# A selective-scan tower on one core: one channel tile's product with B moves from VectorE and GpSimd to TensorE

## What is computed

```python
# D_INNER = 512 channels, D_STATE = 16 states
def step(h, inp):
    dt_t, xv_t, B_t, C_t = inp
    dA = jnp.exp(dt_t[:, :, None] * A[None])
    h = dA * h + (dt_t * xv_t)[:, :, None] * B_t[:, None, :]
    y_t = jnp.einsum('bdn,bn->bd', h, C_t)
    return (h, y_t)
```

## Time and profile before

| | |
|---|---|
| three runs of the kernel | 2601.56, 2601.98, 2603.1 us; median 2601.98 us |
| the profiled execution | 2608.96 us, its span 2607.2 us |
| PE busy | 2079.5 us (80%) |
| DVE busy | 2095.7 us (80%) |
| ACT busy | 1367.9 us (52%) |
| POOL busy | 1210.5 us (46%) |
| scan stage of the first turn | from the first product with B on DVE at 393.61 us to the last gate's start at 604.23 us |

### The profile page before, as it was taken

The page is one execution under the profiler, slowest core; times in us unless marked ns, Lnnn a source line. Parts: engine busy times, 40 slices in busy tenths (PEclk is TensorE's granted clock), DMA queues, the critical chain, the costliest instruction groups (busy, mean ns, idle before and its releaser), DMA issues.

```text
span 2607.2 us, 24235 instructions
## 1 busy us (share of the span) xinstructions
PE 2079.5 (80%) x8436; PEld 1119.4 (43%) x8436; DVE 2095.7 (80%) x2435; ACT 1367.9 (52%) x1914; POOL 1210.5 (46%) x567
## 2 busy tenths in 40 slices
PE   2998886778799887777879898777878988777786
PEld 0326662225433665223542376422353246543244
DVE  6865879996786588999688467999888747799977
ACT  0563456664265446665527544666453744556644
POOL 1220248993222025999222111799722211289952
PEclk9999898999899988899989998899989999888999
DMA  5300000000220000000032000000003100000000
GB/s 182 90 14 1 1 1 1 0 1 0 70 86 1 1 1 0 1 0 0 1 101 55 1 1 1 0 0 0 0 1 118 38 1 1 1 0 0 1 0 17
DMA packets 41073, 51.27 MB, mean 20 GB/s; under 512 B 9072, under 2 KB 32368, under 8 KB 40944
## 3 DMA queue, kind: packets, MB, share of 16 engines
q1 hardware_dynamic: 40944, 49.62, 6.1%
HBM read 26.25 MB, written 10.49 MB: 14 GB/s over the span
## 4 chain that ended last, share of the span: by engine, by line
PE 45%; DVE 25%; POOL 16%; ACT 7%; issue 5%; DMA 1%; SPq 0%; POOLq 0%; DVEq 0%; ACTq 0%
PE psum L988 12%; PE psum L698 10%; POOL big L1985 10%; POOL big L1974 5%; PE psum L845 5%; ACT big L1100 4%; PE psum L833 3%; PE psum L818 3%; PE psum L761 3%; DVE mid L1733 3%; DVE big L1511 2%; DVE mid L1455 2%; PE psum L1003 2%; ACT mid L1100 2%; DVE negmax L1563 2%
## 5 line engine op out<-in xcount | busy, mean ns | idle before, releaser
L988 PE MATMUL psum<-big,ident 128*128 128x512 f32 x992 | 520.6, 674 | 186.0 <-POOL big L1985 185.7
L1835 DVE TENSOR_TENSOR_SCAN big<-psum,b,big 128x512 f32<-128x512 f32 x512 | 618.3, 1277 | 2.3 <-ACT psum L1100 2.0
L1100 ACT ACTIVATE big<-psum 128x1024 f32<-128x1024 f32 (+2 forms) x592 | 448.5, 777 | 229.1 <-PE psum L833 145.1
L1985 POOL TENSOR_TENSOR big<-big 128x2048 f32<-128x2048 f32 x124 | 561.8, 4531 | 9.1 <-DVE big L1835 9.1
L1100 ACT ACTIVATE psum<-mid,aneg 128x512 f32<-128x512 f32 x512 | 353.9, 692 | 251.3 <-DVE big L1835 251.2
L988 PEld LDWEIGHTS psum<-big,ident 128*128 128x128 f32 x992 | 202.0, 213 | 464.2 <-POOL big L1985 243.0
L1563 DVE TENSOR_REDUCE negmax<-psum 128x1 f32<-128x512 f32 x512 | 318.6, 678 | 48.7 <-PE psum L818 47.7
L1974 POOL TENSOR_TENSOR big<-mid,big 128x512 f32<-128x512 f32 (+1 forms) x128 | 224.3, 1753 | 28.2 <-ACT big L1100 28.2
L818 PE MATMUL psum<-mid 96*128 96x512 bf16 x512 | 189.4, 390 | 34.7 <-DMA mid<-mid 23.7
L833 PE MATMUL psum<-mid 98*128 98x512 bf16 x512 | 181.6, 381 | 20.1 <-ACT big L1100 14.2
L1100 ACT ACTIVATE mid<-mid 128x513 f32<-128x513 f32 (+3 forms) x120 | 104.3, 883 | 162.8 <-DVE mid L1845 88.7
(11 more groups left out here) (213 smaller groups left out, 3538.2 us busy)
## 6 DMA issues: line engine op xcount, KB each, us to landing
mid<-mid SPq DMA_DIRECT2D x192, 64.0 KB, 2.5
mid<-scratch SPq DMA_DIRECT2D x192, 64.0 KB, 2.2
scratch<-big SPq DMA_DIRECT2D x4, 1536.0 KB, 5.7
out<-hres SPq DMA_DIRECT2D x8, 513.0 KB, 7.5
big<-in_x SPq DMA_DIRECT2D x8, 512.0 KB, 5.0
big<-in_w SPq DMA_DIRECT2D x2, 1024.0 KB, 6.3
big<-in_wg SPq DMA_DIRECT2D x1, 1024.0 KB, 9.7
big<-in_wu SPq DMA_DIRECT2D x1, 1024.0 KB, 11.5
```

The costliest lines, as they stand in the source:

```text
L988: mm = nc.tensor.matmul(y_psum[:, c], ident[:, :], st(1, k)[:, c], start=(n == 0), stop=(n == NS - 1))
L1100: return nc.scalar.activation(o, a, func, **kw)
L1835: V.tensor_tensor_scan(st(0, k)[:, c], a_psum(DT * k + c), st(0, k)[:, c], b0[:, p, n, c:c + 1], ALU.mult, ALU.add).then_inc(scanned, 1)
L1985: G.tensor_tensor(st(1, k), st(0, k), c_row(k).unsqueeze(1).broadcast_to([P, DT, S]), ALU.mult).then_inc(hc_ready, 1)
```

## The change

For most steps (`by_pe(k)`: all but k = 0, 1, 16, 17 and 31, so 27 of 32) channel tile 3 is handled in another way, and DVE has two tiles of the product with B in each of these steps and POOL one:

- The product of tile 3 with B is made by PE. Once for each sequence PE transposes tile 3 of dt x (`turn_dtx`, four 128x128 transposes into `c_psum`), and ACT copies the result to SBUF (`dtx_t`). For each such step ACT makes four diagonal 128x128 matrices from the identity, scaled with B of 128 tokens (`make_diagonal`), and PE multiplies each transposed block by its diagonal (`multiply_b`) into `c_psum`, which is free once ACT has copied the row of C.
- The scan of tile 3 reads its product from `c_psum`, and its decay from SBUF (`decay_pe`). Only three decays of such a step go through the two PSUM banks.
- `spread_c` of the next step must wait until the scan of tile 3 has read `c_psum`. It is moved behind the first of the four products of `add_y`, and `multiply_b` stands ahead of the last of them.
- The fill `first` also turns B to one column for each state and 128 tokens (eight small products), and ACT copies that (`b_t`).

```diff
+def by_pe(k):
+
+    return k % NS > 1 and k < PAIR * NS - 1
+
+
+PE_STEPS = [k for k in range(PAIR * NS) if by_pe(k)]
+
+IN_BANKS = [DT * k + c for k in range(PAIR * NS) for c in range(DT) if not (by_pe(k) and c == DT - 1)]
...
+            return DT - 2 if by_pe(k) else DT - 1 - k % 2
+
+        def b_end(k):
+            return DT - 1 if by_pe(k) else DT
+
+
+        o_pe = 2 * W8 + 2 * KT * T + 2 * DT * T
+
+        def dtx_t(p):
+            return big[:, o_pe + p * S:o_pe + (p + 1) * S].rearrange("p (q m) -> p q m", q=QT)
+
+        b_t = big[:, o_pe + 2 * S:o_pe + 2 * S + PAIR * QT * NS].rearrange("p (b q n) -> p b q n", b=PAIR, q=QT)
+
+        def diagonal(k):
+            o = (o_pe + 2 * S + PAIR * QT * NS, 6 * W4)[k % 2]
+            return big[:, o:o + S].rearrange("p (q m) -> p q m", q=QT)
+
+        def decay_pe(k):
+            o = 6 * W4 + (1 + k % 2) * S
...
         def a_psum(j):
-            o = (4 + j % 2) * BANK
+            o = (4 + IN_BANKS.index(j) % 2) * BANK
             return psum[:, o:o + BANK]
+
+        def decays(j):
+            return a_psum(j) if j in IN_BANKS else decay_pe(j // DT)
...
+                pe.wait_ge(bc_split, 6 * PAIR)
+                for p in range(PAIR):
+                    for q in range(QT):
+                        o = PAIR * 32 + (QT * p + q) * NS
+                        mm = nc.tensor.matmul(flat_slot("first", 0)[:, o:o + NS], bcp[:, p, 1 + q * P:1 + (q + 1) * P],
+                                              sel[:, 0:NS], start=True, stop=True)
+                mm.then_inc(full[FILLS["first", 0][0]], 1)
...
+                    if k and by_pe(k - 1):
+
+                        pe.wait_ge(scanned, DT * k)
+                    if k % NS == 2:
+                        pe.wait_ge(dtx_turned, k // NS + 1)
                     spread_row(k, NS + k % NS, c_psum).then_inc(c_spread, 1)
 
-                def add_y(k):
+                def add_y(k, c):
                     n = k % NS
-                    pe.wait_ge(hc_ready, k + 1)
-                    for c in range(DT):
-                        if n == 0 and k:
-                            pe.wait_ge(gated, c + 1)
-                        mm = nc.tensor.matmul(y_psum[:, c], ident[:, :], st(1, k)[:, c], start=(n == 0),
-                                              stop=(n == NS - 1))
-                    mm.then_inc(y_summed, 1)
+                    if c == 0:
+                        pe.wait_ge(hc_ready, k + 1)
+                    if n == 0 and k:
+                        pe.wait_ge(gated, c + 1)
+                    mm = nc.tensor.matmul(y_psum[:, c], ident[:, :], st(1, k)[:, c], start=(n == 0), stop=(n == NS - 1))
+                    if c == DT - 1:
+                        mm.then_inc(y_summed, 1)
+
+                def turn_dtx(p, k):
+
+                    pe.wait_ge(c_copied, k + 1)
+                    pe.wait_ge(dtx_ready, p + 1)
+                    for q in range(QT):
+                        mm = nc.tensor.transpose(c_parts[:, q], mid4(p, 3)[:, DT - 1, 1 + q * P:1 + (q + 1) * P],
+                                                 ident[:, :])
+                    mm.then_inc(dtx_full, 1)
+
+                def multiply_b(k):
+
+                    pe.wait_ge(c_copied, k + 1)
+                    pe.wait_ge(diagonals, QT * (PE_STEPS.index(k) + 1))
+                    for q in range(QT):
+                        mm = nc.tensor.matmul(c_parts[:, q], dtx_t(k // NS)[:, q], diagonal(k)[:, q], start=True, stop=True)
+                    mm.then_inc(bx_full, 1)
...
-                    if k + 1 < PAIR * NS:
-                        spread_c(k + 1)
+                    if k % NS == 1:
+                        turn_dtx(k // NS, k)
...
-                        add_y(k - 1)
+                        add_y(k - 1, 0)
+                    if k + 1 < PAIR * NS:
+                        spread_c(k + 1)
+                    if k:
+                        add_y(k - 1, 1)
+                        add_y(k - 1, 2)
+                    if by_pe(k + 1):
+                        multiply_b(k + 1)
+                    if k:
+                        add_y(k - 1, 3)
...
+                run(b_t.rearrange("p b q n -> p (b q n)"),
+                    flat_slot("first", 0)[:, PAIR * 32:PAIR * 32 + PAIR * QT * NS], ACT.Copy).then_inc(b_turned, 1)
...
+                def make_diagonal(k):
+
+                    if k - 2 in PE_STEPS:
+                        act.wait_ge(bx_full, PE_STEPS.index(k - 2) + 1)
+                    for q in range(QT):
+                        run(diagonal(k)[:, q], ident[:, :], ACT.Identity,
+                            scale=b_t[:, k // NS, q, k % NS:k % NS + 1]).then_inc(diagonals, 1)
+
+                act.wait_ge(b_turned, 1)
                 for p in range(PAIR):
                     for n in range(NS):
                         k = NS * p + n
@@ -1313,9 +1401,13 @@
 
                                 act.wait_ge(w_full, 1)
                                 run(mid1(0, 10)[:, 1:T], b_psum, ACT.Copy).then_inc(w_copied, 1)
-                            if j >= 2:
-                                act.wait_ge(scanned, j - 1)
-                            run(a_psum(j), mid4(p, 2)[:, c, 1:T], ACT.Exp,
+                            if j in IN_BANKS:
+                                r = IN_BANKS.index(j)
+                                if r >= 2:
+                                    act.wait_ge(scanned, IN_BANKS[r - 2] + 1)
+                            elif k - 2 in PE_STEPS:
+                                act.wait_ge(scanned, DT * (k - 1))
+                            run(decays(j), mid4(p, 2)[:, c, 1:T], ACT.Exp,
                                          scale=aneg[:, c * NS + n:c * NS + n + 1]).then_inc(decay, 1)
                             if c == 1:
                                 if k == 0:
@@ -1328,6 +1420,11 @@
                                 run(c_row(k), c_psum, ACT.Copy).then_inc(c_copied, 1)
                             if c == (1 if k else 2) and k + 1 < PAIR * NS:
                                 copy_b(k + 1)
+                            if c == 2 and n == 1:
+                                act.wait_ge(dtx_full, p + 1)
+                                run(dtx_t(p), c_parts, ACT.Copy).then_inc(dtx_turned, 1)
+                        if by_pe(k + 1):
+                            make_diagonal(k + 1)
...
+                        bx = st(0, k)[:, c]
+                        if c >= b_end(k):
+                            dve.wait_ge(bx_full, PE_STEPS.index(k) + 1)
+                            bx = c_psum
+                        V.tensor_tensor_scan(st(0, k)[:, c], decays(DT * k + c), bx, b0[:, p, n, c:c + 1],
...
-                    G.tensor_tensor(st(0, k)[:, m:DT], mid4(k // NS, 3)[:, m:DT, 1:T],
-                                    b_row(k).unsqueeze(1).broadcast_to([P, DT - m, S]), ALU.mult).then_inc(b_pool, 1)
+                    G.tensor_tensor(st(0, k)[:, m:b_end(k)], mid4(k // NS, 3)[:, m:b_end(k), 1:T],
+                                    b_row(k).unsqueeze(1).broadcast_to([P, b_end(k) - m, S]), ALU.mult).then_inc(b_pool, 1)
```

14 lines of the change are left out of this document (9 added, 5 removed).

## The result

| | before | changed |
|---|---|---|
| median of the runs | 2601.77 us (4 runs, 2597.68 to 2603.1) | 2573.9 us (4 runs, 2568.16 to 2577.42) |
| profiled execution | 2608.96 us | 2572.49 us, its span 2570.7 us |
| mean granted clock of PE | 0.925 | 0.951 |

The ratio is 0.9886, with a 95% interval of 0.9873 to 0.9899: the changed kernel is 1.1% faster, 27.9 us. The forecast was 2571.

What follows compares the result with a forecast made beforehand. DVE and POOL, both full, were taken to set the pace together. Gains of 7.5 on DVE and 0.9 at the end, less 0.5 at the start, made 7.9 us a turn, 31.6 in all: 2571 us, range 2563 to 2592.

Steps and rivals of the forecast that it cites:

- The step of 5.83 us: Changed steps of the scan: DVE takes 1.11 + 4.72 = 5.83 us and leads; chance 0.71.
- The swapped operands: Scan of tile 3, decay in SBUF and product in PSUM: 1.18 us as before; bound 0.1 us more each, 11 us.
- POOL at 5.73: Changed steps: POOL takes 4.47 + 1.26 = 5.73 us, with 0.1 us of waiting.
- Both engines had to be relieved: Steady scan: DVE at 12.19 and POOL at 12.38 us for two steps both set the pace, so both need relief.
- The term for the small products: PE, eight records of 128x128 products by the diagonals: 1.1 us a step, or 2.0 us slow.
- the rival of the late product: Tile 3's product comes late each step; at 1.35 us of delay 108 steps lose 16 us, about 2587; chance 0.12.
- The clock: PE in steady steps: idle times under 0.5 us, so full clock taken, granted clock 0.95 or more.
- the rival in which PE becomes the bound: PE's waits in changed steps: at granted clock 0.78 a step is 6.4 us, total 2630 us; chance 0.13.
- The sum of a step, 5.1 us: ACT per step: four decays and two copies, 3.9 us, plus four diagonals, 1.2 us; under DVE's 5.83.
- The end: End of a turn: PE's group of y ends 4.0 us after DVE's last product with B, was 5.1; gain 0.9 us.
- The start: Start of a turn, slow first group into y delays the product: 0.5 us a turn charged, bound 2 us.
- The sum: Whole kernel: 7.5 + 0.9 - 0.5 = 7.9 us a turn, four turns 31.6 us.

Runs made afterwards that it cites:

- even steps: Changed kernel with PE making the product of tile 3 only in the even steps (14 a turn): 2589.45 us against 2600.9 before, ratio 0.9943.
- the two halves: PE's product in the even steps alone (2589.45 us) and in the odd steps alone (2595.18 us), each against 2600.9 us before.
- plain order: Changed kernel with the spread of C ahead of all four products into y and the diagonal products behind them: 2621.11 us against 2603.41 before, ratio 1.0066.
- changed again: The changed kernel once more, unedited: 2574.74 us against 2600.9 before, ratio 0.9893.
- odd steps: Changed kernel with PE making the product of tile 3 only in the odd steps (13 a turn): 2595.18 us against 2600.9 before, ratio 0.9966.
- before, filled: Kernel before with five idle bfloat16 products ahead of each spread of C from step 3 on: 2600.97 us against 2600.9, ratio 0.9994.
- before, filled short: Kernel before with the five idle products in the spreads of C of steps 3 to 29 only: 2599.49 us against 2602.22, ratio 0.9986.
- before, tile 0 on POOL: Kernel before with tile 0 as POOL's single tile in even steps and tiles 1 to 3 on DVE: 2611.94 us against 2602.22, ratio 1.0039.
- product last: Changed kernel with the products by the diagonals behind all four products into y: 2570.08 us against 2603.41 before, ratio 0.9876.
- product twice: Changed kernel with PE's eight records of the diagonal products made twice a step: 2574.46 us against 2603.41 before, ratio 0.9889.
- diagonals twice: Changed kernel with ACT making each diagonal twice a step, the extra one unread: 2573.16 us against 2603.41 before, ratio 0.9886.
- two tiles: Changed kernel with tile 2's product with B on PE too, DVE and POOL keeping one tile each: 2571.32 us against 2602.22 before, ratio 0.9882.
- start filled: Changed kernel with ten idle products ahead of a turn's first group into y: 2570.01 us in its one execution.

## Why the prediction was right, point by point

- **The step of 5.83 us.** Right to 0.01 us: 438.17 to 444.00, DVE without idle time, and 11.66 us for two steps against 12.19. DVE sets the step, as the sum of its own parts said. The swapped operands cost nothing.
- **POOL at 5.73.** It had more room, since the single tile is 1.05 us from start to start where nothing waits (451.79 to 452.84 with the even steps alone) and not 1.26. Its waits are 0.24 us and not 0.1. This sets nothing in the changed kernel, but it is the gain of the even steps alone.
- **Both engines had to be relieved.** Shown by the two halves, 12.2 and 10.7 us of stage against 32.9. The prediction let both set the pace, with a step of 6.14 us before. It was DVE's, 12.19 us for two. POOL's lag behind it cost little by itself; POOL had to be relieved because DVE alone would have run into it.
- **PE.** The term for the small products was 1.1 us and measured 0.89: 0.11 a record, not 0.14. So the product was ready 1.45 us ahead, not 1.2, and the rival of the late product had no ground in the order as it is. That the order decides is shown by the plain order, which costs 49 us of stage (860.9 against 811.5).
- **The clock.** 0.99 to 1.00 in the steady stretches, so the rival in which PE becomes the bound fell. The Trainium skill, "TensorE: Matmul & The Clock Gate", A second HAM failure mode, had spoken for it; the short waits of 0.19 and 0.46 us in each step didn't bring the clock down here. Nor is the clock most of the gain: filled by hand in the kernel before, it gave nothing in the steady steps and at best 1.6 us a turn at the end.
- **ACT.** A diagonal was put at 0.3 us and takes 0.29 from start to start, 387 ns as shown. "ScalarE: Activation LUTs", What ACT_TABLE_LOAD costs, in the Trainium skill gives figures from which I estimate 186 + 107 + 93 = 386 ns, and 0.29 us with the overlap; the trace agrees with both estimates. The sum of a step, 5.1 us, was too high all the same: it added decays and copies at their shown durations, and by starts ACT has 4.66.
- **The end.** 3.9 us and not 4.0, against 5.1; less the spread of 0.22 us that is now in PE's run, 1.0 us a turn, where 0.9 was the term. Part of it is that the group no longer runs slow.
- **The start.** 0.53, 0.10, 0.11 and 0.84 us of wait in the four turns, where 0.5 was charged in each.
- **The sum.** 7.9 us a turn were forecast and 8.2 came. From the profiled execution of before the forecast was 2577, and the changed kernel's is 2572.49. The stages came 1.3 us better than the sum of 31.6, and the medians 3.7 us worse. That the median lies only 2.9 us above the forecast is so in part luck.

**What is left.** The medians differ by 27.9 and 26.2 us in the two comparisons, and the stages by 32.9. Outside the stages both kernels have the same instructions, but for the fill `first`. Median less stage, with the stage of the one profiled execution, gives this for the rest of the program:

| kernel | median us | stage us | rest us |
|---|---|---|---|
| before | 2601.77 | 844.4 | 1757.3 |
| changed | 2573.9 | 811.5 | 1762.4 |
| changed again | 2574.74 | 811.5 | 1763.2 |
| even steps | 2589.45 | 832.2 | 1757.2 |
| odd steps | 2595.18 | 833.8 | 1761.4 |
| before, filled | 2600.97 | 842.6 | 1758.3 |
| before, filled short | 2599.49 | 841.6 | 1757.9 |
| before, tile 0 on POOL | 2611.94 | 853.3 | 1758.7 |
| product last | 2570.08 | 815.3 | 1754.8 |
| plain order | 2621.11 | 860.9 | 1760.2 |
| product twice | 2574.46 | 818.6 | 1755.9 |
| diagonals twice | 2573.16 | 812.8 | 1760.4 |
| two tiles | 2571.32 | 808.5 | 1762.8 |
| start filled (one execution) | 2570.01 | 813.8 | 1756.2 |

The rest lies between 1754.8 and 1763.2 us, and among the kernels made from the changed one alone it does so too, with the same code in it. It doesn't go with the length of the stage or with what was edited, and single executions of one kernel lie up to 9 us apart too (2568.16 to 2577.42). The profiled executions alone tell it another way: without their stages they leave 1764.5 us before and 1761.0 and 1763.1 us changed, so in them the rest of the changed kernel is not longer. The profiled execution of before is itself 7 us above the median, and 393.1 us of it lie ahead of the first stage, where the three kernels made from it have 389.4 to 389.8 with the same code there. If the stage is as long in the other executions as in the profiled ones, which only two profiles of the changed kernel bear out, the 5 us lie outside it. Which stretch has them is open: no trace here stands at the median of the kernel before. For the reading of small differences it means that a median can't tell two kernels of 5 us apart, where the stages can: with the product twice the stage is 7 us longer than in the changed kernel, and the median is the same.

## What to carry to other kernels

Where two engines are full to within two in a hundred, count what a change takes from each, step by step: relieving one alone gave about a third of the gain of both. A busy share of 100% on two engines doesn't say which of them sets the pace: here one did, and the other fell behind it step by step. Count the room of a pipelined engine from start to start of its instructions, since shown durations overlap and printed idle times start too late. Where work moves to an in-order engine and shares a buffer there, follow one step through that engine's order; here two calls' place was worth 49 us of stage.

## What was not expected of the hardware

- PE's printed idle time hid 0.43 of 1.07 us of room in a step, ACT's durations of 0.39 us stood 0.29 us apart.
- POOL's product of one 128x512 tile with the row of B takes 1.08 to 1.15 us for tile 2 and 1.25 to 1.40 for tiles 0 and 3, in every kernel here. Open.
- Small float32 products of 128x128 among long ones take 0.11 us a record at a granted clock of 1.00; in the stretch of small products alone they took 0.14.
- Two groups behind idle times of 2.47 and 2.48 us, the same code in two turns, took 3.70 and 5.39 us, with a granted clock of 1.00 just ahead of either: how long the engine was idle doesn't settle by itself how fast it starts.
- Time outside the edited stage varies by 8 us from kernel to kernel with the same code there, as median less stage.
